# A 16-byte tile before, and a 496-byte tile behind, the two split operand tiles of the attention phase

## The reference, cut to what matters

```
q = split_heads(x @ Wq.T); k = split_heads(x @ Wk.T); v = split_heads(x @ Wv.T)
a = einsum('bhnd,bhmd->bhnm', q, k) * scale + (adj + adj)[:, None]
p = softmax(a);  o = einsum('bhnm,bhmd->bhnd', p, v)
x = layernorm(x + o @ Wo.T)
...
support = einsum('bnh,bhk->bnk', x, expert_w[top1])
out = einsum('bnm,bmk->bnk', adj, support)
x = layernorm(x + relu(batchnorm_per_expert(out)))
```

## Time and profile before

| | |
|---|---|
| median of three runs | 2769.57 us |
| the profiled execution: its time, its span | 2769.48 us, 2767.7 us |
| TensorE busy, weight loads busy | 97%, 82% of the span |
| VectorE, ScalarE, GpSimd busy | 69%, 55%, 46% |
| granted TensorE clock, mean | 0.993 |
| mean length of one matmul record, L191 / L200 / L318 / L713 | 284 / 393 to 418 / 389 to 397 / 398 to 420 ns |

### The profile page before, as it was taken

One profiled execution on the slowest core, in us unless ns is written; L12 is line 12 of the kernel. 1 busy time (PEld: TensorE's weight loads), 2 busy tenths in 40 slices (PEclk: granted clock), 3 DMA queues, 4 the chain that ended last, 5 costly groups with the idle time before them and its releaser, 6 DMA issues. The chain is left out here.

```text
span 2767.7 us, 78092 instructions
## 1 busy us (share of the span) xinstructions
PE 2675.1 (97%) x22706; PEld 2277.7 (82%) x22707; DVE 1922.3 (69%) x8351; ACT 1514.3 (55%) x5391; POOL 1282.3 (46%) x1174
## 2 busy tenths in 40 slices
PE   8999999999999999999999999999899999998776
PEld 7898989898989898989888888888788888885232
DVE  6777777777777777777777777777733333335887
ACT  5565656565666666565656565656534444442444
POOL 2334333333434343434333333343356666666887
PEclk9999999999999999999999999999999999999999
DMA  4111111111111111111111111111234444445999
GB/s 147 63 53 54 53 62 53 54 53 62 53 54 53 62 53 54 53 62 53 54 55 60 57 50 58 57 58 49 78 121 136 133 135 135 138 135 199 397 406 349
DMA packets 169428, 277.33 MB, mean 100 GB/s; under 512 B 19378, under 2 KB 52146, under 8 KB 168882
## 3 DMA queue, kind: packets, MB, share of 16 engines
q1 hardware_dynamic: 150962, 243.36, 26.3%
q10 hardware_dynamic: 18432, 33.56, 3.2%
HBM read 184.57 MB, written 92.27 MB: 100 GB/s over the span
## 5 line engine op out<-in xcount | busy, mean ns | idle before, releaser
L564 POOL TENSOR_TENSOR kept<-kept,row_scale 128x512 f32<-128x512 f32 x512 | 533.5, 1042 | 1107.7 <-DVE row_scale L448 1097.9
L342 ACT ACTIVATE kept<-kept,neg_max 128x128 f32<-128x128 f32 x2048 | 795.9, 397 | 138.5 <-DVE neg_max L424 138.5
L424 DVE CUSTOM_DVE_ANT_0 kept<-att_bank,adj_nat 128x128 f32<-128x128 f32 x2048 | 442.6, 286 | 3.5 <-PE att_bank L212 1.6
L342 ACT ACTIVATION_READ_ACCUMULATOR kept<-kept,neg_max 128x1 f32 x2048 | 401.2, 196 | 0.0
L433 DVE TENSOR_REDUCE abs_max<-kept 128x4 f32<-128x512 f32 x512 | 349.2, 682 | 0.1
L191 PE MATMUL att_bank<-xt_hi,w_hi 128*128 128x256 f32 x2048 | 329.8, 284 | 11.0 <-DVE w_lo L401 11.0
L191 PE MATMUL att_bank<-xt_hi,w_lo 128*128 128x256 f32 x2048 | 330.1, 284 | 0.0
L191 PE MATMUL att_bank<-xt_lo,w_hi 128*128 128x256 f32 x2048 | 329.5, 283 | 0.0
L191 PEld LDWEIGHTS att_bank<-xt_hi,w_hi 128*128 128x128 f32 x2048 | 299.3, 191 | 30.5 <-issue 10.6
L375 ACT ACTIVATE kept<-att_bank 128x512 f32<-128x512 f32 x256 | 153.2, 599 | 278.8 <-PE att_bank L255 278.7
L191 PEld LDWEIGHTS att_bank<-xt_hi,w_lo 128*128 128x128 f32 x2048 | 283.2, 192 | 0.0
(11 more groups left out here) (142 smaller groups left out, 5267.8 us busy)
## 6 DMA issues: line engine op xcount, KB each, us to landing
kept<-in_x_t SPq DMA_DIRECT2D x64, 512.0 KB, 3.4
kept<-in_x SPq DMA_DIRECT2D x128, 256.0 KB, 2.6
x_scratch<-kept SPq DMA_DIRECT2D x128, 256.0 KB, 2.0
g_x<-x_scratch SPq DMA_DIRECT2D x128, 256.0 KB, 2.8
n_x<-x_scratch SPq DMA_DIRECT2D x128, 256.0 KB, 7.2
out_x<-n_x ACTq DMA_DIRECT2D x128, 256.0 KB, 5.5
y_scratch<-g_out SPq DMA_DIRECT2D x96, 256.0 KB, 2.0
n_y<-y_scratch SPq DMA_DIRECT2D x96, 256.0 KB, 5.7
```

The source lines that it names most:

```text
L342: nc.scalar.activation(probs[:, h * P:(h + 1) * P], neg_s[:, h * P:(h + 1) * P], ACT.Exp, bias=neg_max[:, h:h + 1], scale=-1.0, accum_out= ...
L424: nc.vector.tensor_tensor_reduce(neg_s[:, h * P:(h + 1) * P], bank[r][:, c * P:(c + 1) * P], adj_nat[:, s], -2.0, BIG, ALU.add, ALU.min, n ...
L564: nc.gpsimd.tensor_tensor(part, part, by, ALU.mult).then_inc(probs_done, 1)
```

## The change

Two tiles are declared that no instruction uses: 4 floats (16 bytes) ahead of `xt_hi`, and 124 floats (496 bytes) behind `xt_lo`.

```
         qk = [half[:, :, :].rearrange("p (w a) (b n) -> p w (a b) n", w=2, n=GN) for half in pair]
+        sb("xt_off", [P, 4])
         xt_hi = sb("xt_hi", [P, 2, C, GN], F32R)
         xt_lo = sb("xt_lo", [P, 2, C, GN], F32R)
+        sb("xt_fill", [P, P - 4])
         adj_nat = sb("adj_nat", [P, UNROLL, P])
         o_hi = sb("o_hi", [P, C, P], F32R)
         o_lo = sb("o_lo", [P, C, P], F32R)
```

## The result

The changed kernel takes 2762.19 us (median of 8 runs, 2759.43 to 2763.58) against 2768.88 for the kernel before on the same chip (8 runs, 2766.90 to 2771.19): the ratio is 0.9976, with a 95% interval of 0.9967 to 0.9985. It is 6.7 us faster, where 12.8 us slower was forecast.

What follows compares the result with a forecast made beforehand. The prediction took TensorE's matmul stream as the bound and added 7.0 us (output product), 5.8 (v) and 0 (q and k), 12.8 in all, to 2769.48 us: 2782 us, 0.5% slower, with a range of 2742 to 2830.

Steps and rivals of the forecast that it cites:

- What bounds the kernel: Attention phase: TensorE's own matmul stream sets the time, 15.33 us a step, 128 steps; no waits hidden behind it.
- That the change does more, and less, than it says: Tile starts: rounding puts xt 32 bytes off W's grid, not 16; the filler misses, so o is 32 off too.
- The 512-column products: Output product (L318) and v (L200): 234 ns a matmul off the grid, costing 7.0 and 5.8 us.
- Y's 234 ns: Expert product, y 96 bytes off W's grid: 234 ns a matmul, taken as the price for L318 and L200.
- the doubt about the register: Expert phase: picking its matrix by a register may have a part in the 234 ns; the row cannot separate them.
- The 256-column products: q and k (L191), 48 matmuls a step at 120 ns: no change taken, 0 us.
- the two bounds: q and k (L191): at most 46 us lost; at best the kernel gains 137 us, 512-column extras included.
- Rival C: L191: sharing the grid costs, so 32 bytes off saves 2.5 ns a matmul; 25.6 us together, 2744; chance 0.24.
- A: L191: q and k pay as well, 127.5 ns a matmul and not 120; 2828 us; chance 0.18.
- B: All products: the address does not matter, y's 234 ns comes from the expert phase itself; 2769.5 us; chance 0.22.
- The other engines: VectorE, ScalarE, GpSimd: casts and o writes cost at most 4 ns a piece more, hidden behind TensorE.

Runs made afterwards that it cites:

- the sweep: Kernel before plus chains of equal matmuls behind the attention loop, one operand read 0 to 496 bytes off; 256 columns 113.3 to 123.4 ns, 512 columns 226.7 to 234.2.

## Why the prediction was wrong

- **What bounds the kernel** was right: TensorE's stream is the attention phase, no wait came or went, and the step's change (0.06 us by the rows shown, 0.054 unrounded) times 128 is about the kernel's.
- **That the change does more, and less, than it says** was right. xt stands 32 bytes off and o goes with it; the run with o back on the grid is 11.1 us faster than the kernel before on its chip, the changed kernel 6.7 on its own, and 4.2 us of that difference stand in the output product.
- **The 512-column products** were right in sign and size: +6.5 against +7.0 and +5.3 against +5.8. Y's 234 ns do come from its distance, as the run with y on the grid shows, so the doubt about the register was not needed. That a price taken 96 bytes off holds at 32 was luck: the sweep has 234.2 and 233.4 there, but 228.9 at 192 bytes and 226.7 at 240, and the prediction had no row to tell.
- **The 256-column products** are the step that failed: "I take nothing". They gave 19.4 us, 3.2 ns for each of 6144 matmuls, more than the 11.8 that v and the output product lost. The reason given was that the unit behind v and the units behind the output product had the same mean of 120 ns. Both stood at the same distance, 0, so their likeness told nothing of another; it was read as a price that does not depend on the rhythm, where the sweep goes from 113.3 to 123.4. The gain lies between the two bounds that the prediction had worked out and then set aside.
- **Rival C** named the place, the direction and the point, 2.1 ns a matmul at L191, from which it decides. With 3.2 it decided. Its price was off, since it let v and the output product settle as well; they lost 11.8 us. Its reason, that the grid is what costs and a start off it parts load and stream, is not borne out as it stands: 96 bytes off, q and k gain nothing (120.1 ns in the sweep), and with 512 columns nothing beats the grid. What in the chip makes the spacing hang on the distance stays open. **A** (L191 slower) falls with the changed kernel's own trace, 117.2 ns a matmul. **B** (no dependence) falls with the sweep and with y; its remark that settling could depend on what ran before is borne out.
- **The other engines** were right: the casts, the minima and the two subtractions keep their lengths to 3 ns.

## What to carry to other kernels

Where TensorE's stream is the bound, the distance in bytes between the stationary and the moving operand is a tuning parameter, worth 1% here without touching an instruction; it has to be chosen for each shape, as the best one for 512 columns was among the worst for 256. It has to be measured in the kernel itself too: at 16 and at 192 bytes the chains by themselves promised more than the kernel gave. Two rhythms with one mean on the same grid are one point, not two: an unknown that no row varies should be left with its bounds, and not be set to zero. Look up where tiles really start before arguing from a declared size.

## What the runs showed that was not expected

Rhythms of one spacing only were seen at 113.3, 116.7 and 120.0 ns with 256 columns, 3.3 ns apart, and at 226.7 and 233.3 with 512, 6.7 ns apart; all others alternate between a few values. Most of the pattern over the distance repeats with 256 bytes. At one distance (192 bytes) the same matmuls kept to 113.4 or to 117.8 ns up to the end of a chain, behind different matmuls; which structure of the memory makes this was not tested.
